# Experts of a two-layer transformer on one core: gate and up as three float32r products in place of one fp32 product

## The chip, the cores and the metric

The kernel runs on 1 core of one Trainium2 chip. The metric is the device time of one execution in microseconds; lower is better. The time before is the median of 3 runs.

## The reference

The whole kernel computes two layers on x of shape 16 x 512 x 128: differential attention, grouped attention with a mixture of experts, eight blocks of linear attention with a feed-forward part, and a ternary feed-forward part. The change touches one step of it, the experts:

```python
topv, topi = jax.lax.top_k(probs, K)          # K = 2 of E = 8 experts for every token
topv = topv / jnp.sum(topv, axis=-1, keepdims=True)
...
g = jnp.einsum('td,edf->etf', flat, Wg)       # d = 128, f = 256
u = jnp.einsum('td,edf->etf', flat, Wu)
a = jax.nn.silu(g) * u
o = jnp.einsum('etf,efd->etd', a, Wd)
moe_out = jnp.einsum('te,etd->td', w, o)
```

All of it is float32.

## The kernel before, in words

The stages run one after the other, with a barrier of all engines between them. `grouped_attention` ends by writing each token's row twice, once for each of its two experts, into a DRAM tensor (`moe_xs`) that is sorted by expert, and a plan: for each of 39 tiles of 512 rows, the row that it starts at and its expert. `expert_tiles` (L1780) works through these 39 tiles (`TILES`) and scatters the results into `moe_ys`; `collect` reads them back.

There is no scheduler: each engine has a program of its own, written out by hand, and an engine runs its instructions in that order. They are tied together by semaphores (`wait_ge` and `then_inc`). A wait holds up all that is queued behind it on its engine.

For a tile j:

- SP (`sp_program`) loads x of the tile (258 KB, `load_x`, L1933) and the three weight matrices of its expert in one DMA (384 KB, `load_w`, L1937). Both have three buffers (XR = 3). `load_w(j + 3)` waits (L1936 and the line before it) until `y_ready` says that tile j's result was copied out, as tile j is then done with its weights.
- TensorE (`pe_program`): `turn(j)` turns x by four transposes of 128 columns (L1832) into the PSUM tile M. `gate_up(j, f)`, for the halves f = 0 and 1, makes gate (k = 0) and up (k = 1), one fp32 matmul of 512 columns each (L1842), into GU. An fp32 matmul stands as two records in the trace, so a tile has 8 records of L1842. `down(j)` makes the third product from the gated values, 8 matmuls of 128 columns in 16 records (L1852), into D. The order is gate_up(j, 0), gate_up(j, 1), turn(j+1), down(j-1).
- ScalarE (`act_program`): `silu(j, f)` of gate (L1874), and `copy_x(j)`, M times the norm's weight into SBUF (xT, two buffers, L1880). The order is silu(j, 0), silu(j, 1), copy_x(j+1).
- VectorE (`dve_program`): `gated(j, f)`, silu times up (L1896, into aT); `address(j)`, the rows to write to as integers (the CAST of L1908); `take(j)`, the COPY of D into y (L1901, three buffers). The order is gated(j, 0), gated(j, 1), address(j), take(j-1). So take(j-1) is the last operation of VectorE's pass j.
- POOL (`pool_program`): four indirect DMAs (L1923) store the four blocks of 128 rows of y.

gate_up(j, 0) waits for x of the tile, for its weights and for gated(j-1, 0). GU holds one tile: both halves of gate and up take four banks of PSUM.

Of the kernel before, what the change touches and what calls it, by code (L numbers as in the profile page):

```python
# [4 lines left out]

F32 = mybir.dt.float32
BF16 = mybir.dt.bfloat16
ALU = mybir.AluOpType
ACT = mybir.ActivationFunctionType
AX = mybir.AxisListType  # L10
# [1769 lines left out]
def expert_tiles(nc, C, R):  # L1780
# [8 lines left out]
    with ExitStack() as ctx:  # L1789
# [10 lines left out]
        w = sb("w", [P, XR, 3, F])  # L1800
        lnw = sb("lnw", [P, 1])
        x = sb("x", [P, XR, NT, ROW])
        xT = sb("xT", [P, 2, SEQ])
        sg = sb("sg", [P, FC, SEQ])
        aT = sb("aT", [P, 2, FC, SEQ])
        y = sb("y", [P, YR, SEQ])
# [7 lines left out]
        lnw_loaded = sem("lnw_loaded")  # L1814
        x_loaded = [sem("x_loaded%d" % k) for k in range(XR)]
        x_turned = sem("x_turned")
        xT_copied = sem("xT_copied")
        gu_filled = sem("gu_filled")
        silu_ready = sem("silu_ready")
        a_ready = sem("a_ready")  # L1820
# [5 lines left out]
        def pe_program(pe):  # L1826
            def turn(j):
                pe.wait_ge(x_loaded[j % XR], 16 * (j // XR + 1))
                if j:
                    pe.wait_ge(xT_copied, j)  # L1830
                for t in range(NT):
                    last = pe.transpose(M[:, t * P:(t + 1) * P], x[:, j % XR, t, 0:P], C["ident"][:, :])  # L1832
                last.then_inc(x_turned, 1)

            def gate_up(j, f):
                if f == 0:
                    pe.wait_ge(xT_copied, j + 1)
                    pe.wait_ge(w_loaded[j % XR], 16 * (j // XR + 1))
                if j:
                    pe.wait_ge(a_ready, FC * (j - 1) + f + 1)  # L1840
                for k in range(2):
                    last = pe.matmul(GU[:, f, k, :], w[:, j % XR, k, f * P:(f + 1) * P],  # L1842
                                     xT[:, j % 2, :], start=True, stop=True)
                last.then_inc(gu_filled, 1)

            def down(j):
                pe.wait_ge(a_ready, FC * j + FC)
                if j >= 2:
                    pe.wait_ge(y_ready, j - 1)
                for t in range(NT):  # L1850
                    for f in range(FC):
                        last = pe.matmul(D[:, j % 2, t * P:(t + 1) * P],  # L1852
                                         aT[:, j % 2, f, t * P:(t + 1) * P],
                                         w[:, j % XR, 2, f * P:(f + 1) * P],
                                         start=(t == 0 and f == 0), stop=(f == FC - 1),
                                         skip_group_check=True)
                last.then_inc(down_filled, 1)

            turn(0)
            for j in range(TILES):  # L1860
                gate_up(j, 0)
                gate_up(j, 1)
                if j + 1 < TILES:
                    turn(j + 1)
                if j:
                    down(j - 1)
            down(TILES - 1)

        def act_program(act):
# [6 lines left out]
            def copy_x(j):  # L1876
                act.wait_ge(x_turned, j + 1)
                if j >= 2:
                    act.wait_ge(gu_filled, FC * (j - 1))
                act.activation(xT[:, j % 2, :], M[:, :], ACT.Copy, scale=lnw[:, 0:1]  # L1880
                               ).then_inc(xT_copied, 1)

            act.wait_ge(lnw_loaded, 16)
            copy_x(0)
            for j in range(TILES):
                silu(j, 0)
                silu(j, 1)
                if j + 1 < TILES:
# [2 lines left out]
        def dve_program(v):  # L1891
# [11 lines left out]
            def address(j):  # L1903
# [3 lines left out]
                    v.wait_ge(y_stored[j % YR], 16 * NT * (j // YR))  # L1907
                v.tensor_copy(dest[:, j % YR, :], x[:, j % XR, :, P]).then_inc(dest_ready, 1)  # L1908

            for j in range(TILES):  # L1910
                gated(j, 0)
                gated(j, 1)
                address(j)
                if j:
                    take(j - 1)
# [1129 lines left out]
```

## Time and profile before

| | |
|---|---|
| median of 3 runs | 3519.7 us (3518.75 to 3526.47) |
| span of the profiled execution | 3506.0 us, 13.7 us less than the median |
| PE busy | 3144.6 us (90%) |
| DVE busy | 2452.0 us (70%) |
| ACT busy | 2276.8 us (65%) |
| POOL busy | 1534.6 us (44%) |
| TensorE's mean granted clock | 0.947 |
| experts stage | from about 1396 to 1663 us |

The time of the profiled execution as a run is not told; its span, from the first to the last instruction, stands for it, and what lies around the span is taken as the 13.7 us to the median. PE is TensorE's matmul, PEld its weight load, DVE VectorE, ACT ScalarE, POOL GpSimd and SP the queue that issues DMAs. A row of a timeline has the start in us, the length in us, engine, line, operation, what it writes and reads, how many operations were merged into the row, and in brackets how long the engine was idle before it and what released it: "issue" means that the profile shows no semaphore, "remote" an event whose sender it doesn't show. In the rows of a window the numbers are its length, then the busy time of each engine with its count of instructions, then the granted clock as a share of full speed (1.00 is 2.4 GHz, 0.50 is 1.2 GHz), the share of time that the DMA engines were busy, and GB/s. A row of waits has who waited for whom, the us in total, the times, and the longest. A row of a group has the us busy in total and, behind it, the mean ns of one.

### The profile page before, as it was taken

What the parts mean: (1) busy time and instruction counts of PE and PEld (TensorE: products, weight loads), DVE (VectorE), ACT (ScalarE), POOL (GpSimd) and SP (SyncE); (2) the same over time, 40 slices, a digit from 0 to 9 for tenths busy, and PEclk for the clock granted to TensorE, in tenths of its full rate; (3) what the DMA queues carried; (4) which work ended last, traced back from release to release, by engine and by line L of the source; (5) the groups of instructions that cost most, each with busy time, mean ns of one, the idle gap of its engine ahead of it and who ended that gap; (6) DMA issues with size and microseconds to landing.
All of it is one profiled execution on the core that took longest, in us unless ns stands there. A gap on an engine that the chain in (4) does not pass through costs nothing. (4 is left out here: it accounts for less than half of the span.)

```text
span 3506.0 us, 72683 instructions
## 1 busy us (share of the span) xinstructions
PE 3144.6 (90%) x22614; PEld 1680.9 (48%) x22614; DVE 2452.0 (70%) x6945; ACT 2276.8 (65%) x3088; POOL 1534.6 (44%) x1807
## 2 busy tenths in 40 slices
PE   6999995898988884987299999999999999999978
PEld 2555552454544452554144444444444444444456
DVE  4666655888777752332678888888888888888754
ACT  4777771555555562222678888888888888888723
POOL 3444442345455523565634333444333444433443
PEclk9999995899999996999599999999999999999989
DMA  4444443222222212443300000000000000000001
GB/s 100 119 118 103 108 100 84 55 61 64 66 53 54 64 40 66 126 142 101 106 7 0 9 0 9 0 9 0 3 6 2 7 0 9 0 9 0 0 16 34
DMA packets 173142, 162.16 MB, mean 46 GB/s; under 512 B 18276, under 2 KB 156735, under 8 KB 172830
## 3 DMA queue, kind: packets, MB, share of 16 engines
q1 hardware_dynamic: 163838, 142.35, 16.7%
q0 software_dynamic: 9088, 16.88, 1.4%
q8 instruction: 142, 2.33, 0.3%
q14 instruction: 74, 0.61, 0.1%
HBM read 92.40 MB, written 68.52 MB: 46 GB/s over the span
## 5 line engine op out<-in xcount | busy, mean ns | idle before, releaser
L546 ACT ACTIVATE ga_PT<-ga_S 128x1024 f32<-128x1024 f32 (+1 forms) x384 | 336.3, 880 | 286.2 <-PE ga_S L373 283.0
L2717 POOL TENSOR_TENSOR lb_y<-lb_ao,XC 128x512 f32<-128x512 f32 x128 | 163.2, 1275 | 807.3 <-ACT lb_ao L2664 807.3
L2556 PE MATMUL lb_H<-lb_x,lb_w 128*128 (+1 forms) x1024 | 513.8, 604 | 0.5 <-issue 0.5
L2565 PE MATMUL lb_FF<-lb_h,lb_w 128*128 128x512 f32 x1024 | 460.3, 592 | 0.0
L2671 ACT ACTIVATE lb_h<-lb_H,lb_prm 128x512 f32<-128x512 f32 x512 | 351.7, 687 | 99.8 <-PE lb_H L2556 84.7
L2763 DVE TENSOR_SCALAR lb_z<-lb_M,lb_mv,lb_rstd 128x128 f32<-128x128 f32 x1024 | 349.9, 404 | 32.8 <-POOL lb_rstd L2708 9.4
L2565 PEld LDWEIGHTS lb_FF<-lb_h,lb_w 128*128 128x128 f32 x1024 | 194.6, 190 | 244.9 <-issue 215.4
L2708 POOL TENSOR_TENSOR lb_rstd<-lb_rstd,half 128x4 f32<-128x4 f32 x256 | 259.5, 1014 | 37.0 <-issue 0.2
L2755 DVE BATCH_NORM_STATS2 lb_stats<-lb_M 128x6 f32<-128x128 f32 x1024 | 228.3, 285 | 30.9 <-PE lb_M L2538 23.0
L2556 PEld LDWEIGHTS lb_H<-lb_x,lb_w 128*128 128x128 f32 x1024 | 174.0, 190 | 132.3 <-issue 122.8
L1521 POOL TENSOR_SCALAR_AFFINE_SELECT da_PT<-da_PT 128x1024 f32<-128x1024 f32 x128 | 146.1, 1146 | 196.3 <-ACT da_PT L1451 196.3
L1456 ACT ACTIVATE da_PT<-da_SY 128x1536 f32<-128x1536 f32 x128 | 185.3, 1447 | 69.3 <-PE da_SY L1326 68.2
L1923 POOL DMA_INDIRECT moe_ys<-moe_y,moe_dest x156 | 153.5, 984 | 123.4 <-DVE moe_y L1901 81.4
L408 PE MATMUL ga_O<-ga_PT,ga_V 128*32 128x128 f32 (+2 forms) x3584 | 204.0, 342 | 0.0
L1338 PE MATMUL da_O<-da_PT,da_V 128*32 128x128 f32 (+2 forms) x3584 | 191.1, 325 | 3.8 <-ACT da_PT L1456 2.3
L764 DVE TENSOR_REDUCE ga_bm<-ga_S 128x8 f32<-128x1024 f32 x128 | 156.2, 1220 | 36.0 <-PE ga_S L397 34.0
L2789 DVE TENSOR_SCALAR lb_x<-lb_M,lb_prm 128x512 f32 (+1 forms) x128 | 103.6, 810 | 106.3 <-PE lb_M L2524 106.3
L2653 ACT ACT_TABLE_LOAD x130 | 166.8, 1283 | 2.3
L767 DVE TENSOR_REDUCE ga_bm<-ga_S 128x8 f32<-128x1024 f32 x128 | 155.9, 1218 | 17.5 <-remote 10.1
L1842 PE MATMUL moe_GU<-moe_xT,moe_w 128*128 128x512 f32 x312 | 143.3, 602 | 26.9 <-issue 23.4
L397 PE MATMUL ga_S<-ga_kT,ga_qT 48*128 48x128 bf16 (+2 forms) x1792 | 142.9, 254 | 27.0 <-ACT ga_PT L546 24.4
L373 PE MATMUL ga_S<-ga_qT,ga_kT 51*128 51x128 bf16 (+2 forms) x1792 | 140.4, 250 | 29.5 <-DVE ga_bm L764 28.0
(330 smaller groups left out, 7087.7 us busy)
## 6 DMA issues: line engine op xcount, KB each, us to landing
moe_w<-experts_dram SPq DMA_DIRECT2D x39, 384.0 KB
da_qT<-da_stq SPq DMA_DIRECT2D x64, 192.0 KB, 4.3
da_kT<-da_stk SPq DMA_DIRECT2D x64, 192.0 KB, 5.2
ga_qT<-ga_stq SPq DMA_DIRECT2D x32, 384.0 KB, 6.0
moe_x<-moe_xs SPq DMA_DIRECT2D x39, 258.0 KB
tc_g<-moe_ys SPq DMA_DIRECT2D x32, 256.0 KB, 3.2
da_stq<-da_parts SPq DMA_DIRECT2D x16, 384.0 KB, 2.4
da_stk<-da_parts SPq DMA_DIRECT2D x16, 384.0 KB, 3.1
```

Source lines behind the costliest of these rows:

```text
L408: last = pe.matmul(O[32 * c:32 * c + 32, q0:q0 + cols], V[:, (n // 4) % BUF, j, n % 4, :], PT[:, (2 * n + c // 2) % RING, c % 2, o:o + col ...
L546: act.activation(PT[:, n % RING, :, lo:hi], score_banks(u)[:, :, 0:hi - lo], ACT.Exp, scale=SCALE).then_inc(probs, 1)
L1338: last = pe.matmul(O[32 * c:32 * c + 32, q0:q0 + cols], V[:, (n // 4) % 2, j, 2 * (n % 4) + c % 2, :], PT[:, (2 * n + c // 2) % RING, c % ...
L1456: act.activation(PT[:, n % RING, :, 512:HEAD_COLS], SY[:, :, :].rearrange("p a n -> p (a n)").rearrange("p (i n) -> p i n", i=2), ACT.Exp, ...
L2556: pe.matmul(H[:, k % 2, :], w1[:, k, :], x1_of(i), start=True, stop=True).then_inc(h_filled, 1)
L2565: pe.matmul(FF[:, :], w2[:, k, :], h[:, k, :], start=(k == 0), stop=(k == KC - 1)).then_inc(ff_filled, 1)
L2653: act.preload_act_table_set("gelu_apprx_tanh_and_others")
L2671: act.activation(h[:, k, :], H[:, k % 2, :], ACT.Gelu_apprx_tanh, bias=col(FB1 + k, i)).then_inc(h_ready, 1)
L2708: pool.tensor_tensor(out[:, :], out[:, :], C["half"][:, 0:NT], ALU.pow).then_inc(done, 1)
L2717: pool.tensor_tensor(y1[:, :], ao[:, :], state(i), ALU.add).then_inc(y1_ready, 1)
L2755: v.bn_stats(stats[:, t, :], M[:, t * P:(t + 1) * P])
L2763: last = v.tensor_scalar(z[:, t, :], M[:, t * P:(t + 1) * P], mv[:, t, 0:1], rstd[:, t:t + 1], ALU.subtract, ALU.mult)
```

## The change

Gate and up are no longer one fp32 product each. x and the two weight matrices are written as a high part, of the type float32r, and the rest, and the product is the sum of three float32r products: high x high, rest of w x high, high x rest of x. They add up in PSUM. ScalarE makes the high parts (copy_x as before, now with a float32r output; the new copy_w, 128 x 512 for gate and up together), VectorE the rests (the new rest_of_w and rest_of_x). The new tile wp has two buffers of both parts. copy_w(j+1) and rest_of_w(j+1) stand first in ScalarE's and VectorE's pass j, rest_of_x(j+1) behind gated(j, 1). TensorE waits for them in place of the weights' load. down, the loads and the stores stay as they are.

```diff
--- before.py
+++ after.py
@@ -5,6 +5,7 @@
 
 F32 = mybir.dt.float32
 BF16 = mybir.dt.bfloat16
+F32R = mybir.dt.float32r
 ALU = mybir.AluOpType
 ACT = mybir.ActivationFunctionType
 AX = mybir.AxisListType
@@ -1800,7 +1801,8 @@
         w = sb("w", [P, XR, 3, F])
         lnw = sb("lnw", [P, 1])
         x = sb("x", [P, XR, NT, ROW])
-        xT = sb("xT", [P, 2, SEQ])
+        xT = sb("xT", [P, 2, 2, SEQ], F32R)
+        wp = sb("wp", [P, 2, 2, 2, F], F32R)
         sg = sb("sg", [P, FC, SEQ])
         aT = sb("aT", [P, 2, FC, SEQ])
         y = sb("y", [P, YR, SEQ])
@@ -1814,7 +1816,10 @@
         lnw_loaded = sem("lnw_loaded")
         x_loaded = [sem("x_loaded%d" % k) for k in range(XR)]
         x_turned = sem("x_turned")
-        xT_copied = sem("xT_copied")
+        xT_high_ready = sem("xT_high_ready")
+        xT_low_ready = sem("xT_low_ready")
+        w_high_ready = sem("w_high_ready")
+        w_low_ready = sem("w_low_ready")
         gu_filled = sem("gu_filled")
         silu_ready = sem("silu_ready")
         a_ready = sem("a_ready")
@@ -1827,20 +1832,28 @@
             def turn(j):
                 pe.wait_ge(x_loaded[j % XR], 16 * (j // XR + 1))
                 if j:
-                    pe.wait_ge(xT_copied, j)
+                    pe.wait_ge(xT_low_ready, j)
                 for t in range(NT):
                     last = pe.transpose(M[:, t * P:(t + 1) * P], x[:, j % XR, t, 0:P], C["ident"][:, :])
                 last.then_inc(x_turned, 1)
 
             def gate_up(j, f):
+                s = j % 2
+                cols = slice(f * P, (f + 1) * P)
                 if f == 0:
-                    pe.wait_ge(xT_copied, j + 1)
-                    pe.wait_ge(w_loaded[j % XR], 16 * (j // XR + 1))
+                    pe.wait_ge(w_low_ready, j + 1)
+                    pe.wait_ge(xT_high_ready, j + 1)
                 if j:
                     pe.wait_ge(a_ready, FC * (j - 1) + f + 1)
                 for k in range(2):
-                    last = pe.matmul(GU[:, f, k, :], w[:, j % XR, k, f * P:(f + 1) * P],
-                                     xT[:, j % 2, :], start=True, stop=True)
+                    for part in range(2):
+                        pe.matmul(GU[:, f, k, :], wp[:, s, part, k, cols], xT[:, s, 0, :],
+                                  start=(part == 0), stop=False)
+                if f == 0:
+                    pe.wait_ge(xT_low_ready, j + 1)
+                for k in range(2):
+                    last = pe.matmul(GU[:, f, k, :], wp[:, s, 0, k, cols], xT[:, s, 1, :],
+                                     start=False, stop=True)
                 last.then_inc(gu_filled, 1)
 
             def down(j):
@@ -1877,12 +1890,22 @@
                 act.wait_ge(x_turned, j + 1)
                 if j >= 2:
                     act.wait_ge(gu_filled, FC * (j - 1))
-                act.activation(xT[:, j % 2, :], M[:, :], ACT.Copy, scale=lnw[:, 0:1]
-                               ).then_inc(xT_copied, 1)
-
+                act.activation(xT[:, j % 2, 0, :], M[:, :], ACT.Copy, scale=lnw[:, 0:1]
+                               ).then_inc(xT_high_ready, 1)
+
+            def copy_w(j):
+                act.wait_ge(w_loaded[j % XR], 16 * (j // XR + 1))
+                if j >= 2:
+                    act.wait_ge(gu_filled, FC * (j - 1))
+                act.activation(wp[:, j % 2, 0, :, :], w[:, j % XR, 0:2, :], ACT.Copy
+                               ).then_inc(w_high_ready, 1)
+
+            copy_w(0)
             act.wait_ge(lnw_loaded, 16)
             copy_x(0)
             for j in range(TILES):
+                if j + 1 < TILES:
+                    copy_w(j + 1)
                 silu(j, 0)
                 silu(j, 1)
                 if j + 1 < TILES:
@@ -1907,9 +1930,28 @@
                     v.wait_ge(y_stored[j % YR], 16 * NT * (j // YR))
                 v.tensor_copy(dest[:, j % YR, :], x[:, j % XR, :, P]).then_inc(dest_ready, 1)
 
+            def rest_of_w(j):
+                v.wait_ge(w_high_ready, j + 1)
+                v.tensor_tensor(wp[:, j % 2, 1, :, :], w[:, j % XR, 0:2, :],
+                                wp[:, j % 2, 0, :, :].bitcast(F32), ALU.subtract
+                                ).then_inc(w_low_ready, 1)
+
+            def rest_of_x(j):
+                v.wait_ge(xT_high_ready, j + 1)
+                v.scalar_tensor_tensor(out=xT[:, j % 2, 1, :], in0=M[:, :], scalar=lnw[:, 0:1],
+                                       in1=xT[:, j % 2, 0, :].bitcast(F32), op0=ALU.mult,
+                                       op1=ALU.subtract).then_inc(xT_low_ready, 1)
+
+            rest_of_w(0)
+            v.wait_ge(lnw_loaded, 16)
+            rest_of_x(0)
             for j in range(TILES):
+                if j + 1 < TILES:
+                    rest_of_w(j + 1)
                 gated(j, 0)
                 gated(j, 1)
+                if j + 1 < TILES:
+                    rest_of_x(j + 1)
                 address(j)
                 if j:
                     take(j - 1)
```

## Rows read from the trace of the kernel before

**Rows 1.** Windows: us; busy of PE, PEld, DVE, ACT, POOL; clock; DMA share; GB/s.

```profile
1411.00:1654.00 243.00, 214.57 (x1048) 139.15 (x1046) 82.13 (x150) 65.29 (x110) 146.79 (x150) 1.00 0.45 132
```

**Rows 2.** Timeline of POOL: start, length, what ended its idle time; stores, and the last.

```profile
1464.17 0.98 POOL L1923 DMA_INDIRECT moe_ys<-moe_y,moe_dest  x1 [2.98 <-DVE moe_y L1901]
1465.46 0.98 POOL L1923 DMA_INDIRECT moe_ys<-moe_y,moe_dest  x1 [0.30 <-issue]
...
1477.13 0.98 POOL L1923 DMA_INDIRECT moe_ys<-moe_y,moe_dest  x1 [2.96 <-DVE moe_y L1901]
...
1661.54 0.98 POOL L1923 DMA_INDIRECT moe_ys<-moe_y,moe_dest  x1 [0.30 <-issue]
```

**Rows 3.** Timeline of PE: products, turn and down of a tile, and products of others.

```profile
1398.30 5.10 PE L1842 MATMUL moe_GU<-moe_xT,moe_w 128*128 128x512 f32 x8 [0.84 <-ACT moe_xT L1880]
...
1467.36 3.67 PE L1842 MATMUL moe_GU<-moe_xT,moe_w 128*128 128x512 f32 x8 [1.50 <-issue]
1470.87 0.60 PE L1832 MATMUL moe_M<-ident,moe_x 128*128 128x128 f32 x4
1471.31 1.95 PE L1852 MATMUL moe_D<-moe_w,moe_aT 128*128 128x128 f32 x16
1473.09 3.60 PE L1842 MATMUL moe_GU<-moe_xT,moe_w 128*128 128x512 f32 x8
...
1481.03 3.67 PE L1842 MATMUL moe_GU<-moe_xT,moe_w 128*128 128x512 f32 x8 [2.11 <-issue]
...
1557.83 3.67 PE L1842 MATMUL moe_GU<-moe_xT,moe_w 128*128 128x512 f32 x8 [1.19 <-issue]
```

**Rows 4.** SP's own waits in the stage.

```profile
SPq L1936 <- DVE moe_y L1901: 140.0, 32, 7.7
```

**Rows 5.** Timeline of DVE: the COPY of L1901 in five tiles; gated, then CAST.

```profile
1404.06 0.69 DVE L1896 TENSOR_TENSOR moe_aT<-moe_GU,moe_sg 128x512 f32<-128x512 f32 x1 [1.02 <-ACT moe_sg L1874]
1404.67 0.16 DVE L1908 CAST moe_dest<-moe_x 128x4 uint32<-128x4 f32 x1
...
1410.62 0.69 DVE L1901 COPY moe_y<-moe_D 128x512 f32<-128x512 f32 x1 [0.83 <-PE moe_D L1852]
...
1462.64 0.69 DVE L1901 COPY moe_y<-moe_D 128x512 f32<-128x512 f32 x1 [3.15 <-remote]
...
1475.61 0.69 DVE L1901 COPY moe_y<-moe_D 128x512 f32<-128x512 f32 x1 [3.14 <-remote]
...
1553.45 0.69 DVE L1901 COPY moe_y<-moe_D 128x512 f32<-128x512 f32 x1 [3.26 <-remote]
...
1642.07 0.69 DVE L1901 COPY moe_y<-moe_D 128x512 f32<-128x512 f32 x1 [0.74 <-PE moe_D L1852]
```

**Rows 6.** Timeline of SP: the first weight load, and the one after a COPY.

```profile
1395.18 0.37 SPq L1937 DMA_DIRECT2D moe_w<-experts_dram  x1
...
1464.08 0.34 SPq L1937 DMA_DIRECT2D moe_w<-experts_dram  x1
```

**Rows 7.** Timeline of ACT: the second silu and the copy of x of one tile.

```profile
1463.68 0.60 ACT L1874 ACTIVATE moe_sg<-moe_GU 128x512 f32<-128x512 f32 x1 [0.37 <-PE moe_GU L1842]
1464.17 0.68 ACT L1880 ACTIVATE moe_xT<-moe_M,moe_lnw 128x512 f32<-128x512 f32 x1
```

**Rows 8.** Groups of instructions by line and form, whole span (second number: mean ns).

```profile
L2240 ACT ACTIVATE ff_xT<-ff_M 128x512 f32<-128x512 f32 x16 | 9.5, 592 | 8.1 <-PE ff_M L2196 8.1
...
L2800 DVE SCALAR_TENSOR_TENSOR lb_fq<-lb_Q,lb_prm,lb_eq 128x512 f32<-128x512 f32 x128 | 96.1, 751 | 26.6 <-issue 26.2
...
L2071 DVE TENSOR_TENSOR tc_acc<-tc_acc,tc_g 128x512 f32<-128x512 f32 x16 | 11.1, 693 | 1.2
```

**Rows 9.** Timeline of PE in another stage: 128 columns of bf16, one full row group.

```profile
1294.42 0.40 PE L271 MATMUL ga_M<-identb,ga_mp 128*48 128x128 bf16 x4
```

**Rows 10.** Windows of another stage; the clock stands behind the busy times.

```profile
1039.40:1042.70 3.30, 1.03 (x4) 0.10 (x2) 2.16 (x2) 0.99 (x2) 2.45 (x3) 1.00 0.13 41
1042.75:1046.15 3.40, 3.36 (x33) 1.98 (x34) 3.21 (x6) 1.45 (x3) 1.16 (x1) 0.50 0.00 0
```

## The prediction

> **What bounds the kernel now.** I read the windows first. The experts stage is 265 of the 3506 us, and the change touches nothing else. In its steady part TensorE is busy 214.6 of 243 us at the full clock, POOL 147, VectorE 82, ScalarE 65 [rows 1]: nobody is full, so something makes them wait in turn. The timeline of POOL gives the beat: the first store of every second tile starts 12.96 us after the one two tiles earlier (1464.17, 1477.13), so a tile costs 6.48 us; from the COPY of tile 0 (1410.62) to that of tile 36 (1642.07) it is 231.45 / 36 = 6.43 us [rows 2, 5].
>
> TensorE's own work is less: from the start of a tile's products to that of the next 1473.09 - 1467.36 = 5.73 us, of which the products take 3.51, the turn 0.44, down 1.78 [rows 3]. In every second tile it stands idle ahead of the products (1.50 and 2.11 us) and the releaser is not told. The timelines tell it: of the products at 1467.36, x was ready at 1464.85 (the ACT copy, 1464.17 + 0.68) [rows 7], so the weights remain. Their load was issued at 1464.08 [rows 6], behind the COPY of y that ended at 1463.33 [rows 5]. SP waits 140 us in the stage for that COPY [rows 4]. With three buffers the load of tile j+2 waits until tile j-1 is taken out. The delay from the end of the COPY to the first product is **D = 4.03 us** (1463.33 to 1467.36); of the 17 such tiles the shortest is 3.69 (1554.14 to 1557.83) and the longest 4.73 (1476.30 to 1481.03) [rows 3, 5].
>
> **The change, part by part.**
>
> *Products.* Four fp32 products of 512 columns take 3.51 us, 0.88 each. They become twelve float32r ones, and the trace has no float32r. Bound above: they cost as fp32, 12 x 0.88 = 10.5 us. Bound below: four bf16 matmuls of 128 columns over all 128 rows fit in 0.40 us [rows 9], so 0.10 per 128 columns at most and 0.40 per 512 (4.8 us for twelve); how far under that it goes is open. I take the lower end, since an operand that isn't full fp32 is nearer to the bf16 row than to the fp32 one. As will be seen any price up to 0.47 us changes nothing but the tail.
>
> The Trainium skill ("FP8 and Floating Point Precision", TensorE Precision Notes) says that true fp32 goes through the array in four passes (high and low halves crossed) and that reduced-precision fp32 is read as 22 bits. By that, I estimate, twelve single passes stand against sixteen, 2.6 us against 3.5, so TensorE would save 0.9 us a tile, 34 us in all. No row here shows it.
>
> *The copy of w.* One Copy of 128x512 per tile on ScalarE, 0.59 us (as L2240) [rows 8], where a second operation follows 0.49 us after the first starts [rows 7].
>
> *The rests.* One TENSOR_TENSOR (0.69) and one SCALAR_TENSOR_TENSOR (0.75) per tile on VectorE [rows 8]. As totals they hide: ScalarE has 65 + 39 x 0.6, VectorE 82 + 39 x 1.44 of 243 us. No DMA is added, the descriptors on POOL are the same.
>
> *The new wait.* This decides. copy_w(j+1) stands ahead of silu(j, 0), and rest_of_w(j+1) ahead of gated(j, 0). Before, the weights of j+1 were wanted when TensorE came to tile j+1; now ScalarE and VectorE stand still for them before they may finish tile j. But load_w(j+1) waits for the COPY of tile j-2, which is the last thing in VectorE's pass j-1. So the load starts only as pass j starts, everything in pass j is queued behind it, and pass j ends with the COPY that allows the next load. It is a closed ring:
>
> - end of COPY to the weights there: 4.00 (D less the 0.03 in which TensorE starts)
> - copy_w on ScalarE 0.59, and 0.03 until VectorE starts
> - rest_of_w, gated 0, gated 1: 0.61 each, as an operation on VectorE follows the one before when it need not wait (1404.06 to 1404.67) [rows 5]: 1.83. The two silus (0.5 and 0.6 behind copy_w) are ready in time.
> - rest_of_x 0.67 (0.75 less the same overlap); its input is ready at 4.00 + 0.49 x 3 + 0.68 = 6.15, the engine at 6.45
> - the CAST 0.10, the COPY 0.69 (down, which it waits for, was released a pass earlier)
>
> Sum **7.9 us per tile**. TensorE needs 12 x 0.40 + 0.44 + 1.78 = 7.0 at most beside it, and stays hidden up to (7.9 - 2.22) / 12 = 0.47 us a product; POOL needs 4 x 1.29 = 5.2 (1464.17 to 1465.46) [rows 2]. Cover gone, each would show as its excess over 7.9.
>
> Bounds of the ring: shortest D and 0.1 us less in each of two overlaps, 3.66 + 3.9 - 0.2 = 7.4; full durations of all operations (0.69 x 3, 0.75, 0.16), 8.3; with the longest D too, 9.0. A stall goes, and what is late next is VectorE's pass itself.
>
> *The sum.* The loads with a COPY ahead of them are those of tiles 3 to 38, so 36 passes: 36 x (7.9 - 6.43) = +53. Head: weights of tile 0 are issued at 1395.18 [rows 6] and land some 3.3 us later, copy_w and rest_of_w follow, products start near 1399.7 and not at 1398.30 [rows 3] (+1.4); the cheaper products and no full ring in tiles 0 and 1 give back some 2.4: -1. Tail: the last store now starts 18.8 us after the COPY of tile 36 ended (1642.76 to 1661.54) [rows 2, 5], since POOL then works off two tiles and more; in the new order POOL has caught up, and three tiles of stores follow that COPY within 0.8 + 12 x 1.29 = 16.3 us, ended, against 19.8: -3.5. Sum +48.5. The median is 3519.7; the profiled span is 3506.0, and the 13.7 us around it don't change. 3519.7 + 48.5 = **3568 us**.
>
> **The rivals.**
>
> *A: the weights come in time, and the beat becomes that of TensorE or POOL (faster).* By the Trainium skill's four-pass rule (same page) the products would shrink enough for it. The place is copy_w. With D short, a pass is the larger of TensorE's 2.22 + 12 products, which is 5.5 if one costs 0.27, under the bound of 0.40 [rows 9], and POOL's 5.2 plus some of the 0.8 from the COPY's end to the first store (1463.33 to 1464.17) [rows 2, 5]; about 5.5: 36 x (5.5 - 6.43) = -33, 3486 us. It decides below D = 5.5 - 3.9 = 1.6 us; the shortest of 17 is 3.69 [rows 3, 5]. Only another reading of the ring could bring it. 6%.
>
> *B: the ring is there but costs no more than today's beat.* The 12.96 us for two tiles hold a COPY that comes late in one of them; its idle 3.14 us (released by "remote") I can't explain [rows 5]. If that wait is what today's time consists of, and it goes, the ring would need 6.4: no row allows it. 3520 us, 4%.
>
> *C: float32r costs as fp32.* TensorE then needs 10.5 + 2.22 = 12.7 us a tile and is the bound: 38 x (12.7 - 6.43) = +238, 3758 us. For it: nothing in the trace excludes it. Against: the trace's other operands that aren't fp32 cost less per column [rows 9]. 5%.
>
> *D: the clock falls.* In the ring TensorE idles about 3 us of 7.9. In another stage a window of 3.30 us in which it was busy 1.03 was followed by 3.40 us at 0.50, the 1.2 GHz level [rows 10]. Half the time at 1.2 GHz makes 4.8 into 7.2 us, still under 7.9; always at 1.2 GHz makes 9.6 and a beat of 9.6: 36 x 3.2 = +114, 3630 us. A TensorE busy all the time should not be slowed, so the true case lies between. 6%.
>
> **How the numbers follow.** The ring has 79%, with 3550 (7.4) to 3583 (8.3) as its inner bounds and 3608 with the longest D (9.0). A measurement of this kernel tells about 0.2% (7 us) from no change. Faster: A and a little for what I overlooked, 0.07. Same: B, 0.04. Slower: 0.89. The range reaches from 3542 to 3612: it leaves out A, B, C and D, and some of the ring's own edge.
>
> **What would show it.** In the changed profile: the waits of ScalarE before L1874 or the new Copy should be some 3 us each tile, with the copy of w starting within 0.1 us of the landing and about 4.0 us behind the end of the COPY of y; the COPY of y should come every 7.9 us, evenly, not in pairs; TensorE's share in the stage should fall to some 60 to 70%, with products about 0.2 to 0.4 us apart and x468 records, if one each. SP's wait for the COPY should remain. Wrong, if the COPYs come under 6.5 us apart (A or B), if products stand 0.8 us apart (C), or if the clock in the stage's windows reads 0.50 throughout (D).

## The result, and the profile after

The change makes the kernel slower: 3564.12 us (3563.09 to 3566.43, 4 runs) against 3522.23 us (3518.75 to 3526.47, 4 runs) of the kernel before on the same chip, a ratio of 1.0119 [1.0104, 1.0133]. Predicted were 3568 us and a range from 3542 to 3612.

The page of the changed kernel, its span, its busy times and two groups:

```profile
span 3561.4 us, 73150 instructions
PE 3146.3 (88%) x22770; PEld 1722.5 (48%) x22770; DVE 2502.3 (70%) x7023; ACT 2291.6 (64%) x3127; POOL 1539.1 (43%) x1807
L1965 POOL DMA_INDIRECT moe_ys<-moe_y,moe_dest x156 | 161.2, 1034 | 164.6 <-DVE moe_y L1924 125.3
L1900 ACT ACTIVATE moe_wp<-moe_w 128x512 fp32r<-128x512 f32 x39 | 24.5, 629 | 232.3 <-DMA moe_w<-experts_dram 232.3
```

No engine has got much more to do: against the page of before, PE has 1.7 us more, ScalarE 15, VectorE 50 in a span that is 55 us longer. What is new is the last number: ScalarE stands 232.3 us in front of the copy of the weights, waiting for their load. The waits of the stage (1398 to 1710 us) show who stands behind it, and SP's own waits close the circle:

```profile
ACT moe_wp L1900 <- DMA moe_w<-experts_dram: 232.3, 38, 25.6
DVE moe_wp L1935 <- ACT moe_wp L1900: 159.7, 33, 14.4
POOL moe_ys L1965 <- DVE moe_y L1924: 125.3, 36, 27.3
```

```profile
SPq L1978 <- DVE moe_y L1924: 192.2, 35, 6.2
```

ScalarE waits for the load, VectorE for ScalarE, SP (which issues the load) for VectorE's COPY of y; SP's wait was 140.0 us before [rows 4]. The steady part of the stage, as windows, against [rows 1]:

```profile
1411.00:1690.00 279.00, 207.51 (x1149) 171.09 (x1148) 115.35 (x215) 79.08 (x144) 142.58 (x137) 0.94 0.37 111
```

TensorE is busy 74% of it, not 88%, and the clock is granted at 0.94, so part of the stretch ran at the lower of its two levels. One pass of the ring, from one COPY of y to the next, as the timeline shows it:

```profile
1474.14 0.69 DVE L1924 COPY moe_y<-moe_D 128x512 f32<-128x512 f32 x1
...
1475.57 0.34 SPq L1979 DMA_DIRECT2D moe_w<-experts_dram  x1
...
1478.62 0.63 ACT L1900 ACTIVATE moe_wp<-moe_w 128x512 fp32r<-128x512 f32 x1 [5.49 <-DMA moe_w<-experts_dram]
1479.15 1.06 ACT L1887 ACTIVATE moe_sg<-moe_GU 128x512 f32<-128x512 f32 x2
1479.28 0.69 DVE L1935 TENSOR_TENSOR moe_wp<-moe_w,moe_wp 128x512 fp32r<-128x512 f32 x1 [4.45 <-ACT moe_wp L1900]
1479.52 1.31 POOL L1965 DMA_INDIRECT moe_ys<-moe_y,moe_dest  x1 [0.30 <-issue]
1479.89 1.28 DVE L1919 TENSOR_TENSOR moe_aT<-moe_GU,moe_sg 128x512 f32<-128x512 f32 x2
1480.11 0.69 ACT L1893 ACTIVATE moe_xT<-moe_M,moe_lnw 128x512 fp32r<-128x512 f32 x1
...
1480.89 1.16 PE L1850 MATMUL moe_GU<-moe_xT,moe_wp 128*128 128x512 f32 x4 [2.35 <-ACT moe_xT L1893]
1481.09 0.74 DVE L1941 SCALAR_TENSOR_TENSOR moe_xT<-moe_M,moe_lnw,moe_xT 128x512 fp32r<-128x512 f32 x1
1481.74 0.16 DVE L1931 CAST moe_dest<-moe_x 128x4 uint32<-128x4 f32 x1
1481.81 0.69 DVE L1924 COPY moe_y<-moe_D 128x512 f32<-128x512 f32 x1
...
1483.86 0.60 PE L1837 MATMUL moe_M<-ident,moe_x 128*128 128x128 f32 x4
```

This is the ring of the prediction (the circle of waits in which each pass waits for the one before) in its order: COPY ends (1474.83), load, copy of w (1478.62), rest of w (1479.28), the two gated products, rest of x (1481.09), CAST, COPY. The bracket of 5.49 us before ScalarE's copy is the idle time that the load ended; all that VectorE does afterwards follows without a gap. TensorE starts the products of the next tile after 2.35 us of idle time, finishes all twelve in 1483.86 - 1480.89 = 2.97 us, 0.25 us each, and waits again. The ends of the stage:

```profile
1405.21 1.11 PE L1837 MATMUL moe_M<-ident,moe_x 128*128 128x128 f32 x4 [25.11 <-DMA moe_x<-moe_xs]
...
1419.83 0.69 DVE L1924 COPY moe_y<-moe_D 128x512 f32<-128x512 f32 x1 [0.17 <-PE moe_D L1865]
...
1703.37 0.68 DVE L1924 COPY moe_y<-moe_D 128x512 f32<-128x512 f32 x1
...
1719.04 0.98 POOL L1965 DMA_INDIRECT moe_ys<-moe_y,moe_dest  x1 [0.31 <-issue]
```

From the COPY of tile 0 to that of tile 36 are 283.54 us, 7.88 us a tile (before 231.45 and 6.43 [rows 5]). From the first turn to the end of the last store the stage takes 314.8 us; it took 266.2, its first turn starting at 1396.34. That is +48.6.

### The profile page after: what moved, and what is told of

The parts are those of the page before. It is cut to its first block and busy times, and to the rows that moved or that the text cites. A ratio compares the mean times of both kernels' runs of the same rounds, so it can differ in the third digit from the quotient of the medians.

```text
span 3561.4 us, 73150 instructions
## 1 busy us (share of the span) xinstructions
PE 3146.3 (88%) x22770; PEld 1722.5 (48%) x22770; DVE 2502.3 (70%) x7023; ACT 2291.6 (64%) x3127; POOL 1539.1 (43%) x1807
## 5 line engine op out<-in xcount | busy, mean ns | idle before, releaser
L1965 POOL DMA_INDIRECT moe_ys<-moe_y,moe_dest x156 | 161.2, 1034 | 164.6 <-DVE moe_y L1924 125.3
L1900 ACT ACTIVATE moe_wp<-moe_w 128x512 fp32r<-128x512 f32 x39 | 24.5, 629 | 232.3 <-DMA moe_w<-experts_dram 232.3
```

## The experiments

Twelve runs, in three groups of four, each group on a chip of its own (e9, e10 and e11 are kernels that had run before on another chip). The kernel before ran in every group, and its time differs between the chips by more than the change's effect, so only ratios and beats are compared across them. Chip 1 is the one of the result above; that the first profile of the kernel before was taken there too isn't on record. The table gives the beat, from the start of the COPY of tile 0 to that of tile 36 divided by 36, the shortest and the longest of these 36 passes, and the length of the stage, from the first turn to the end of the last store. All starts are from the timelines.

| kernel | chip | COPY 0, COPY 36 | beat | shortest, longest | stage | ratio to the kernel before |
|---|---|---|---|---|---|---|
| before | 1 | 1410.62, 1642.07 | 6.43 | 3.0, 10.0 | 266.2 | |
| the change | 1 | 1419.83, 1703.37 | 7.88 | 7.5, 8.5 | 314.8 | 1.0119 |
| e1 copies last | 2 | 1414.47, 1680.37 | 7.39 | 7.2, 8.3 | 302.0 | 1.0079 |
| e2 four weights | 2 | 1419.11, 1662.64 | 6.76 | 3.1, 11.6 | 278.8 | 1.0028 |
| e3 wait alone | 2 | 1410.58, 1650.10 | 6.65 | 6.1, 8.1 | 271.0 | 1.0008 |
| e4 before, four weights | 2 | 1414.76, 1645.09 | 6.40 | 2.0, 10.2 | 262.3 | 0.9987 |
| e5 one product | 3 | 1393.44, 1679.51 | 7.95 | 7.7, 8.5 | 316.3 | 1.0233 |
| e6 rest before take | 3 | 1403.22, 1622.62 | 6.09 | 5.8, 6.6 | 252.4 | 1.0051 |
| e7 half the stores | 3 | 1424.51, 1604.77 | 5.01 | 5.0, 5.7 | 206.9 | none (one run, with a step added) |
| e8 e6 and four weights | 3 | 1392.78, 1601.09 | 5.79 | 5.8, 6.1 | 241.6 | 1.0015 |
| e9 before, again | 4 | 1397.09, 1600.87 | 5.66 | 5.7, 5.7 | 235.5 | |
| e10 the change, again | 4 | 1388.28, 1672.73 | 7.90 | 7.5, 8.5 | 315.7 | 1.0240 |
| e11 four weights, again | 4 | 1392.09, 1579.99 | 5.22 | 3.1, 6.7 | 220.1 | 0.9950 |
| e12 rest of w first | 4 | 1393.25, 1593.49 | 5.56 | 5.5, 6.0 | 237.6 | 1.0007 |

The median of the kernel before was 3522.23 us on chip 1, 3511.57 on chip 2, 3461.67 on chip 3 and 3456.23 on chip 4.

**e1: the copy and the rest of w last in their passes.**

```diff
 (ScalarE) for j:
-    copy_w(j + 1)
     silu(j, 0); silu(j, 1); copy_x(j + 1)
+    copy_w(j + 1)
 (VectorE) for j:
-    rest_of_w(j + 1)
     gated(j, 0); gated(j, 1); rest_of_x(j + 1); address(j); take(j - 1)
+    rest_of_w(j + 1)
```

> The changed kernel with the same instructions in another order: copy_w(j+1) behind copy_x(j+1) on ScalarE, rest_of_w(j+1) behind take(j-1) on VectorE. Theory (a ring of one pass through the in-order queues: COPY, weight load, copy_w, silu, gated, rest_of_x, COPY): the weights' wait now has only work of the next tile behind it, the ring spans two passes: 3.8 load + 0.63 + 0.7 + 3.0 products + 0.44 turn + 1.78 down + 0.7 COPY = 11.1 us for two tiles, 5.6 a tile against 7.88; 36 x -2.3 = -82, about 3482 us, below the kernel before. Rival (what costs is the added work of copies and rests, or the float32r products, wherever they stand): no change, 3560 to 3566 us.

Measured: 3539.42 us, ratio 1.0079 [1.0064, 1.0093], a beat of 7.39. The load's ring was opened, but another took its place, as the timeline of this kernel shows:

```profile
1488.71 0.69 DVE L1923 COPY moe_y<-moe_D 128x512 f32<-128x512 f32 x1 [0.24 <-PE moe_D L1865]
1489.31 0.68 DVE L1934 TENSOR_TENSOR moe_wp<-moe_w,moe_wp 128x512 fp32r<-128x512 f32 x1
...
1490.05 1.20 PE L1850 MATMUL moe_GU<-moe_xT,moe_wp 128*128 128x512 f32 x4 [1.38 <-DVE moe_wp L1934]
...
1492.93 0.60 PE L1837 MATMUL moe_M<-ident,moe_x 128*128 128x128 f32 x4
...
1493.36 1.95 PE L1865 MATMUL moe_D<-moe_w,moe_aT 128*128 128x128 f32 x16
1495.94 0.69 DVE L1923 COPY moe_y<-moe_D 128x512 f32<-128x512 f32 x1 [0.75 <-PE moe_D L1865]
```

The rest of w stands behind the COPY of down's result; the products of the next tile need that rest, and the next down stands behind those products on TensorE, and the next COPY waits for it: 0.60 + 0.74 + 2.88 + 0.43 + 2.58 = 7.23 us, with no load in it. Of the last 2.58 us down takes 1.95; the other 0.63 lie between its end and the COPY, no instruction explains them, and they stand in 30 of the 39 tiles. Six of the 36 passes take 8.2 us, and there the clock is what is added. In the windows of this kernel around the products of such a pass, which last 4.16 us in place of 2.88, it is granted at 0.67, so in part at the lower level:

```profile
1437.50:1441.70 4.20, 4.17 (x13) 3.17 (x14) 0.69 (x1) 0.60 (x1) 3.07 (x4) 0.67 0.62 177
```

In this ring TensorE's products are a link, in that of the change they aren't. The expectation had followed the ring it meant to open, and not the one that the new place of rest_of_w closes.

**e2: four buffers for the weights, nothing else.**

```diff
+    WR = 4
-        w = sb("w", [P, XR, 3, F])
+        w = sb("w", [P, WR, 3, F])
...
 (SP) load_x(j + XR) as before; behind y_ready of tile j:
-                    load_w(j + XR)
+                    load_w(j + WR)
```

> The changed kernel with four weight buffers in place of three, so a load is issued a pass earlier. Theory: ScalarE finds the weights there, the ring opens, and the bound is TensorE (2.97 + 0.44 + 1.78 = 5.2 us a tile) or POOL's four stores (5.16): 5.4 a tile, 36 x -2.5 = -89, about 3475 us. Rival (added work or products cost): 3560 to 3566 us. Rival (the load itself is too slow, DMA bandwidth): little gain, over 3540.

Measured: 3522.79 us, ratio 1.0028 [1.0016, 1.0041]. This confirms the ring: with one buffer more the same instructions in the same order cost a quarter of what the change had cost on chip 1 (e10 and e11 make the same comparison on one chip). The expected beat of 5.4 and 3475 us did not come, though: it also shows that the ring is not all, since the beat of 6.76 us is uneven and far from the 5.2 that TensorE and POOL need. The timeline of this kernel shows waits that no instruction explains:

```profile
1479.74 0.63 PE L1856 MATMUL moe_GU<-moe_xT,moe_wp 128*128 128x512 f32 x2
...
1482.03 0.60 ACT L1888 ACTIVATE moe_sg<-moe_GU 128x512 f32<-128x512 f32 x1 [3.02 <-PE moe_GU L1856]
...
1487.16 0.69 DVE L1925 COPY moe_y<-moe_D 128x512 f32<-128x512 f32 x1 [1.38 <-remote]
```

The silu waits only for the products that end at 1480.37, and starts 1.66 us later; one pass earlier the same silu started at 1475.40, 0.03 us after products that ended at 1475.37. I call these **late signals**.

**e3: the wait alone, in the kernel before.**

```diff
 (ScalarE) for j:
+                if j + 1 < TILES:
+                    act.wait_ge(w_loaded[(j + 1) % XR], 16 * ((j + 1) // XR + 1))
                 silu(j, 0)
```

> The kernel before with nothing but ScalarE's wait for the next tile's weights put ahead of silu(j, 0): no copies, no rests, fp32 products. Theory: the ring closes here too, but has less work on it: 4.0 + 0.49 + 0.60 + 0.03 + 0.61 + 0.10 + 0.69 = 6.5 us a tile against 6.43, so +3 us, between 0 and +12 (3522 to 3534). Then the price of the change is the 1.3 us of copies and rests that stand on the ring. Rival (the early wait alone costs it all): +42, 3564 us.

Measured: 3513.28 us, ratio 1.0008 [0.9999, 1.0016]. On this chip the early wait for the weights costs next to nothing by itself. The ring is there: ScalarE waits 174.5 us for the loads, in the waits of this kernel,

```profile
ACT moe_sg L1874 <- DMA moe_w<-experts_dram: 174.5, 35, 6.6
```

and the beat has become even, 6.65. But what stands behind the load here, a silu, two gated products, CAST and COPY, sums to little more than the beat that was there. So on this chip the price of the change is what it puts on the ring. Where the kernel before has a shorter beat (5.66 in e9), the early wait would have a price of its own, an estimated 36 x (6.65 - 5.66) = 36 us; e3 was not run there. In the pass of the changed kernel shown above the first gated product starts 1479.89 - 1478.62 = 1.27 us after the load has ended, where a silu of 0.60 alone would let it start after some 0.63; the rest of x adds 0.65. That is 1.3 us, and the beats differ by 7.88 - 6.65 = 1.23.

**e4: four weight buffers in the kernel before.** The edit of e2 in the kernel before.

> The kernel before with four weight buffers. Theory: TensorE's idle time in every second tile is the late weight load; with it gone the tile costs TensorE's 5.73 us, 36 x -0.7 = -25, about 3497 us. Rival (the idle time comes from something else, such as the COPY of y that starts 2.4 us late in every second tile): no change, 3518 to 3526 us.

Measured: 3504.29 us, ratio 0.9987 [0.9976, 0.9999]. Had the weights' lateness been what TensorE loses in the kernel before, 25 us were to be had. 7 were there, and at most 8 by the interval. The wait that stays in this kernel's list is

```profile
DVE moe_y L1902 <- remote: 57.0, 20, 4.3
```

and it was in the kernel before as well, "DVE moe_y L1901 <- remote", 54.7 us in 18 waits. It is the late signal again: down of [rows 3] ends at 1471.31 + 1.95 = 1473.26, and the COPY that waits for it and nothing else starts at 1475.61 [rows 5], 2.35 us later.

**e5: one product in place of three.**

```diff
                 for k in range(2):
-                    for part in range(2):
-                        pe.matmul(GU[:, f, k, :], wp[:, s, part, k, cols], xT[:, s, 0, :], ...)
+                    last = pe.matmul(GU[:, f, k, :], wp[:, s, 0, k, cols], xT[:, s, 0, :], ...)
...
-                for k in range(2):
-                    last = pe.matmul(GU[:, f, k, :], wp[:, s, 0, k, cols], xT[:, s, 1, :], ...)
```

> Edit: the change, with only the product of the two high parts: the eight correction products of a tile are left out (all copies and rests stay), so gate and up have the high parts alone. Theory (TensorE isn't what sets the beat of this stage; the ring of load, copy and rest of the weights, gated, rest of x, take does): the beat stays at 7.8 to 7.9 us a tile, the stage within 5 us of the change's 314.8, and the ratio to the kernel before stays 1.010 to 1.013. Rival (the twelve products set the beat): eight products at 0.25 us less a tile, 39 x 2.0 = 78 us less, ratio near 0.99.

Measured: 3541.11 us, a beat of 7.95, a stage of 316.3 us. Its windows:

```profile
1411.00:1690.00 279.00, 183.07 (x848) 152.10 (x846) 112.49 (x209) 75.39 (x138) 145.92 (x143) 0.76 0.38 108
```

Two thirds of the products are gone, and nothing is gained; e10, on another chip, has 7.90 and 315.7 with all of them. Even the clock's fall to 0.76 in this stretch costs nothing that shows. The ratio, 1.0233 [1.0212, 1.0254], is not the expected 1.010 to 1.013, because the kernel before is quicker on this chip; e10 shows that.

**e6: the copy of w behind the copy of x, the rest of w between address and take.**

```diff
 (ScalarE) silu(j, 0); silu(j, 1); copy_x(j + 1)
+    copy_w(j + 1)
 (VectorE) gated(j, 0); gated(j, 1); rest_of_x(j + 1); address(j)
+    rest_of_w(j + 1)
     take(j - 1)
```

> Edit: the change, with the copy of the next tile's weights behind the copy of the next x on ScalarE, and its rest between the address and the take on VectorE. The gated products and the rest of x then stand no longer between the weights' arrival and the take that starts the next load, so the ring is load to copy 3.8 + copy 0.63 + step 0.03 + rest 0.70 + take 0.69 = 5.9 us. Theory of one ring: a beat of 5.9 to 6.6 us a tile (36 x 1.3 to 2.0 us less than the change, so 3482 to 3507 us against 3511.6 of the kernel before on this chip, ratio 0.992 to 0.999). Rival (the second ring of the earlier experiment: rest of the weights, products 2.9, turn 0.4, down 1.9, take 0.7 = 6.0 with no load in it, plus late signals of TensorE where GpSimd issues stores in long runs): a beat of 6.4 to 7.0, ratio 0.999 to 1.004.

Measured: 3479.74 us, ratio 1.0051 [1.0033, 1.0069], a beat of 6.09, where the ring's sum was 5.9 to 6.6. Two instructions moved, no buffer added, and 7.9 has become 6.1. The kernel is still 18 us slower than the one before. The ratio expected for it (0.992 to 0.999) took chip 2's beat of before and chip 3 has a shorter one.

**e7: four weight buffers and half the stores.**

```diff
 (POOL) for each tile:
-                for t in range(NT):
+                for t in range(2):
                     pool.indirect_dma_start(...)
```

> Edit: the change with four weight buffers, and GpSimd stores only two of the four blocks of each tile's result (half the results are left out; the rows are filled once from another tensor in a step of its own before the stage, which costs some 50 us outside the tiles). Theory (in the run with four weight buffers TensorE's signals came 1.5 to 6 us late where GpSimd issued eight or more scattered stores without a gap): with at most 2.6 us of stores a tile GpSimd never falls behind, no signal is late, and the beat falls from 6.77 to 5.2 to 5.7 us a tile. Rival (the lateness has nothing to do with the stores, or the beat is set by something else): the beat stays at 6.5 to 7.0 and the late signals stay.

This kernel leaves out half of the stores and ran once (3460.05 us, with the step that fills the rows), so only its beat is used. It is 5.01 us and even, no signal is late, and TensorE has become the bound, busy in 169.50 of 170 us in the windows of this kernel:

```profile
1430.00:1600.00 170.00, 169.50 (x1088) 150.39 (x1087) 115.84 (x205) 81.60 (x136) 66.78 (x68) 1.00 0.57 157
```

That looked like a proof that the stores make the signals late. It was none: the comparison was with e2, and that had run on another chip. e11 repeats e2 on a chip that, like this one, has no late signals.

**e8: e6 and four weight buffers.**

> Edit: both at once: four weight buffers, and copy and rest of the next tile's weights behind the copy and rest of x. No load stands on a ring. Theory of the late signals: GpSimd's stores, 5.2 us a tile, come in long runs, and the beat stays at 6.4 to 6.9, as in the run with four weight buffers alone: ratio 1.000 to 1.004. Rival (that run's remaining loss was the order on ScalarE and VectorE): a beat of 5.4 to 6.0, ratio 0.985 to 0.993.

Measured: 3464.3 us, ratio 1.0015 [1.0005, 1.0026], a beat of 5.79, the same in 35 of 36 passes. POOL issues 113 stores here with no gap over 0.6 us, and not one signal is late. So long runs of stores don't delay the signals by themselves; whether they do on a chip that has late signals is not shown. The beat is the one that the rival named (5.4 to 6.0), the ratio is not (0.985 to 0.993): that was worked out from the slower kernel before of chip 2. What the beat consists of is in the timeline:

```profile
1505.76 0.60 ACT L1888 ACTIVATE moe_sg<-moe_GU 128x512 f32<-128x512 f32 x1 [0.79 <-PE moe_GU L1856]
...
1506.39 0.69 DVE L1919 TENSOR_TENSOR moe_aT<-moe_GU,moe_sg 128x512 f32<-128x512 f32 x1 [0.69 <-ACT moe_sg L1888]
...
1507.00 0.74 DVE L1941 SCALAR_TENSOR_TENSOR moe_xT<-moe_M,moe_lnw,moe_xT 128x512 fp32r<-128x512 f32 x1
...
1507.73 0.69 DVE L1935 TENSOR_TENSOR moe_wp<-moe_w,moe_wp 128x512 fp32r<-128x512 f32 x1
1507.93 1.34 POOL L1965 DMA_INDIRECT moe_ys<-moe_y,moe_dest  x1 [0.30 <-issue]
...
1508.47 1.20 PE L1851 MATMUL moe_GU<-moe_xT,moe_wp 128*128 128x512 f32 x4 [0.52 <-DVE moe_wp L1935]
```

Silu of the second half, gated, rest of x, rest of w, and only then the products of the next tile, 3.05 us more until the next silu: a ring between three engines, without a load.

**e9: the kernel before, again.**

> No edit: the kernel before, looked at once more, beside the three runs below on the same chip. Its first profile had a span of 3506.0 us, and the times of its other runs were 13 to 20 us longer; the change's profile had 1.7 us around its span. Theory (the first profiled execution was a quick one, and nothing lies around the span but 2 us): time less span is 1.5 to 2.5 us here too. Rival (before has 13 us around its span): 12 to 15 us. And as the comparison for the stage: a beat of 6.3 to 6.6 us a tile with TensorE's late signals (copies of the down product 1.7 us or more after its end) in about half of the tiles, on any chip; or 6.1 or less with none, if the late signals belong to some chips only.

Its time is 3461.31 us and its span 3459.2: 2.1 us lie around the span. And this chip shows a different kernel before. In the timeline:

```profile
1502.19 0.60 PE L1832 MATMUL moe_M<-ident,moe_x 128*128 128x128 f32 x4
...
1502.63 1.95 PE L1852 MATMUL moe_D<-moe_w,moe_aT 128*128 128x128 f32 x16
...
1504.41 3.60 PE L1842 MATMUL moe_GU<-moe_xT,moe_w 128*128 128x512 f32 x8
1504.62 0.69 DVE L1901 COPY moe_y<-moe_D 128x512 f32<-128x512 f32 x1 [0.58 <-PE moe_D L1852]
```

The COPY starts 0.04 us after down's end, the products follow without a gap, and the windows have TensorE busy all of the time:

```profile
1411.00:1570.00 159.00, 159.00 (x786) 103.72 (x785) 67.20 (x113) 49.69 (x84) 109.91 (x112) 1.00 0.54 158
```

The beat is 5.66 us, near the 5.73 of TensorE's own work that the prediction read off [rows 3]. With no late signals the weights are in time with three buffers.

**e10: the change, again.**

> No edit: the change, on the chip of these runs, so that the run with one product (7.95 us a tile on another chip than the change's 7.88) has its like. Theory (one ring through load, copies, gated and take): a beat of 7.8 to 8.0 us whatever the chip, ratio 1.010 to 1.024, the higher end where the kernel before is quick. Rival (the run with one product lost something of its own): 7.8 or less with a ratio near 1.012 on a chip where the kernel before takes 3460.

Measured: 3538.2 us, ratio 1.0240 [1.0225, 1.0256], a beat of 7.90. The changed kernel has the same ring on both chips (7.88, 7.90); the kernel before has not. Here the change costs 36 x (7.90 - 5.66) = 81 us, and the stage is 80.2 us longer. By the beats of e3, measured on chip 2, some 36 of them would be the early wait and the rest what stands behind it.

**e11: four weight buffers, again** (the kernel of e2).

> No new edit: the change with four weight buffers, again, beside the next. With half the stores its beat was an even 5.0 us a tile with no late signal; with all of them on an earlier chip 6.77 and uneven. Theory (the stores cause it, on every chip): 6.4 to 6.9 us, uneven, with late signals. Rival (the chip of the earlier run caused it): an even 5.2 to 5.6, set by GpSimd's four stores of 1.29 us, ratio 0.980 to 0.990.

Measured: 3441.31 us, ratio 0.9950 [0.9934, 0.9965], a beat of 5.22. POOL issues all 156 stores with no gap over 0.6 us, and no signal is late. So the rival holds in its cause, the chip and not the stores alone, and in the mean beat; the passes are not even (3.1 to 6.7 us), and the gain is smaller than its 0.980 to 0.990. Against e10, the same kernel with one weight buffer less on the same chip, it is 97 us: the whole loss, and some more. 5.22 is four times POOL's store, in the groups of this kernel

```profile
L1966 POOL DMA_INDIRECT moe_ys<-moe_y,moe_dest x156 | 156.6, 1004 | 74.9 <-issue 46.0 <-DVE moe_y L1925 28.9
```

1.004 us and 0.30 between two. So on chip 4 the change with one buffer more is 0.5% faster than the kernel before, POOL being the bound. On chip 2 it was not (1.0028), and the best there was e4.

**e12: four buffers, the copy of w behind that of x, the rest of w ahead of the rest of x.**

```diff
 (VectorE) against e8:
     gated(j, 0); gated(j, 1)
+    rest_of_w(j + 1)
     rest_of_x(j + 1); address(j)
-    rest_of_w(j + 1)
     take(j - 1)
```

> Edit: the change with four weight buffers, the copy of the next weights behind the copy of x on ScalarE, and on VectorE gated, gated, rest of w, rest of x, address, take. In the run with the rest of w behind the rest of x, the beat was an even 5.79, the ring products 3.05, silu 0.6, gated 0.7, rest of x 0.74, rest of w 0.69, and start. Theory (that ring): the rest of x, 0.74, leaves the ring, since only the third part of the products waits for it; the beat falls to 5.2 to 5.4, where TensorE's own work (5.0) and GpSimd's stores (5.2 and what they are stretched by) end, and stays even: ratio to the kernel before 0.99 or less (about 17 us under the 1.0015 of that run: 0.995 to 0.997 if the chip is as quick as that one). Rival (late signals come as soon as the order lets TensorE run ahead of the stores): 6.2 to 6.9 and uneven.

Measured: 3455.95 us, ratio 1.0007 [0.9996, 1.0018], a beat of 5.56, even; a beat of 5.2 to 5.4 and a ratio of 0.995 to 0.997 were expected. The rest of x left the ring, but ScalarE's copy of w, behind which VectorE now has to wait, entered it:

```profile
1507.97 0.69 DVE L1919 TENSOR_TENSOR moe_aT<-moe_GU,moe_sg 128x512 f32<-128x512 f32 x1 [0.67 <-ACT moe_sg L1888]
1508.41 0.63 ACT L1901 ACTIVATE moe_wp<-moe_w 128x512 fp32r<-128x512 f32 x1
...
1509.07 0.69 DVE L1935 TENSOR_TENSOR moe_wp<-moe_w,moe_wp 128x512 fp32r<-128x512 f32 x1 [0.40 <-issue]
```

VectorE is idle for 0.40 us until the copy is done; 0.74 less 0.40 would be 0.34, and 0.23 were gained, 5.79 to 5.56 (e8 ran on chip 3). With four weight buffers, on the chips without late signals, the change's own order, copy and rest of w first (e11), is the best of the three that were tried; with three buffers it is the worst.

## Why the prediction was right

**The ring.** Right, in its place and its size. Term by term, as the mean of the 36 passes: end of COPY to the copy of w 3.99 us (taken 4.00), copy of w to its rest 0.66 (0.62), rest and both gated products 1.81 (1.83), rest of x 0.66 (0.67), CAST 0.07 (0.10), COPY 0.68 (0.69), together 7.88, where 7.9 was predicted. Only the first varies much, from 3.62 to 4.63; the pass shown above has 3.79 and takes 7.67 us. e11 opens the ring with one more buffer and gets the whole loss back on its chip, e2 most of it on another, e6 takes the gated products and the rest of x off the ring and gets 6.09, e5 shows that the products don't count.

**The sum.** The passes gave 283.54 - 231.45 = +52.1 (predicted +53). The head, first turn to first COPY, was 14.28 and is 14.62 us, +0.3 (-1). The tail, from the start of the COPY of tile 36 to the end of the last store, was 20.45 and is 16.65, -3.8 (-3.5). Together +48.6, where +48.5 was predicted.

**The products.** They take 0.25 us each. The bounds were 0.88 and 0.40, and 0.40 was taken: mis-sized, but without effect, as said, under 0.47. The Trainium skill ("FP8 and Floating Point Precision", TensorE Precision Notes), by which twelve single passes would take an estimated 2.6 us a tile against 3.5 of fp32, was nearer: the trace has 2.97 against 3.51 [rows 3]. In e11, where neither ring nor late signals stand in the way, the shorter products count: TensorE needs 5.0 us (e7) and no longer 5.66 (e9).

**What lies around the span.** Wrong. "The profiled span is 3506.0, and the 13.7 us around it don't change": only 1.7 us lie around the changed kernel's span, and 2.1 around that of before (e9). So the first profiled execution must have taken some 3508 us, 14 less than the median of its kernel and 10 less than the quickest of its four runs. It may have been a quick one or on another chip (the runs of the kernel before on chip 2 take 3504 to 3518 us); the record doesn't tell. The spans differ by 55.4 us and the medians by 41.9. Of the 55.4 the experts are 48.6; their first turn starts 8.9 us later, behind stages that the change doesn't touch, and what follows them is 2 us shorter. By the medians the change cost 42 us and not 48.5, and where the other 6 or 7 us are isn't shown. The median of before, taken as 3519.7, is 3522.2 with its fourth run. The two errors run against each other, so that the total came within 4 us is partly luck.

**The reading of the kernel before.** Half right. "So the weights remain": in those tiles they may well have been the last to come, but not as the cause. The COPY that starts their load was late, by the idle 3.14 us "that I can't explain", and e4, which takes the weights out of it, gains only 0.13%. The steps of the ring came out right since they were measured from the COPY's end, so the late signals didn't enter. They entered the difference: with them the beat of before is 6.43, and where they are missing it is 5.66. On chip 4 the same prediction would have been some 33 us too low (81 against 48.5).

**The rivals.** A (weights in time) did not come with three buffers, but is what e11 is: it predicted a beat of 5.5, and 5.22 was measured. B took the "remote" wait for today's time, and that much was right; the ring just needs 7.9 and not 6.4. C is refuted by 0.25 us a product. D: the clock did fall, to 0.94 in the stage's windows, and cost nothing that shows, as in e5 at 0.76. The prediction's prices for D were wrong in themselves: 7.2 and 9.6 us are the products alone, without the 2.22 us of turn and down, so by its own 0.40 us a product even half the time at the lower level would have gone past 7.9; and 36 x 3.2 us on top of 3519.7 are 3634, not 3630. At the measured 0.25 us it would not have.

**The signs named beforehand** came for the most part: COPYs every 7.5 to 8.5 us and no longer in pairs, the copy of w on average 4.0 us behind the COPY's end, 468 records of products, SP's wait for the COPY. Two were missed: TensorE's share is 74%, above the 60 to 70% given, and ScalarE waits 5.7 us on average in front of the copy of w, not some 3 us.

## What to carry to other kernels

If a wait is moved to the front of an engine's pass, and the load it waits for is released by the last operation of that pass, all that stands between them is now in series with the load, once per pass. The wait alone can be free where the kernel is no faster for another reason (e3 on chip 2), and then each operation added behind it has its full price. Draw the ring, sum it, and ask for each place a new operation could have which ring it closes: the same operations gave 7.9, 7.4, 6.1 and (with a fourth buffer, on a chip without late signals) 5.2 us a tile. A difference between two kernels holds only for the chip on which both ran: here the same pair gave 1.0119 and 1.0240, and two of my theories rested on runs of different chips.

## What was not expected of the hardware

The chips differ. On chips 1 and 2 ScalarE and VectorE often see the end of a TensorE operation 1.7 us late or more (18 of the 39 COPYs in the first profile of the kernel before, by its waits, 20 in e4, and silus in e2), on chips 3 and 4 in none of the eight runs; the kernel before takes 3512 to 3522 us on the former and 3456 to 3462 on the latter, over 4, 25, 13 and 15 runs. Not every kernel has them there: the change has one, at its last COPY (1.58 us), e3 two, near its end (1.34 and 1.50 us), and e1 none over 0.7 us. Long runs of stores alone don't make them (e8 has 113 stores in a row, e11 all 156, both without one). Matmul ends in a trace are modelled, so what exactly is late isn't shown. The cause stays open; that stores make them likelier on a chip that has them was not tried. Each chip was used in one session, so that something else differed between the sessions can't be excluded.

A float32r product of 512 columns takes 0.25 us, an fp32 one 0.88. And POOL's store takes up to 1.50 us in place of 0.98 where the rest of w runs beside it, an operation of VectorE that reads and writes SBUF alone (the rows at 1479.52 in the change and at 1507.93 in e8 have 1.31 and 1.34); over all stores of the change the mean is 1.034 us against 0.984 in the kernel before. The order of the two starts decides. In the change the rest of w began 0.05 to 0.42 us ahead of the store in 21 cases, and each of these stores lasted longer, by the time that the two ran together less 0.12 to 0.13 us (0.33 of 0.45 us in the row at 1479.52). In 19 cases it began later than the store, or less than 0.03 us before, and in none did the store last longer; nor did any of the stores that ran without it, though gated products or rests of x ran beside some of them. The Trainium skill ("SBUF — State Buffer", SBUF: two separate sides) says that VectorE and GpSimd share a pair of ports by an exclusive lock, which the one that starts first holds for its whole instruction, and that an operation of VectorE with two inputs in SBUF takes it, against a GpSimd operation that reads SBUF. The trace agrees for the stores that start second. It doesn't for the other order: the rest of w that starts second is not held up for the store's 0.98 us, but takes 0.74 us at most, 0.69 as a rule. It was not tested by itself.
